# Later x batches load behind the shared weights, high halves move a slot back, batch work is spread over slots, routing in other operations, list values multiplied by GpSimd

## What is computed

```python
def _L0_xattn_ref(x, adj, W, b):          # x is ctx, adj is layernorm(x)
    si = jnp.einsum('bnd,d->bn', x, Wi[0])
    sj = jnp.einsum('bnd,d->bn', x, Wj[0])
    xij = jax.nn.sigmoid(si[:, :, None] + sj[:, None, :] + b[0])
    return P_ASEM * xij + (1.0 - P_ASEM) * adj
...
    probs = jax.nn.softmax(x @ gate_w.T, axis=-1)
    vals, idx = jax.lax.top_k(probs, K)                    # 4 of 16 experts
    w = vals / jnp.sum(vals, axis=-1, keepdims=True)
    ...
    w_gu = dequant_fp4(gate_up_packed, gate_up_scales)
    act = swiglu(jnp.einsum('th,ehi->eti', x, w_gu))
    y_e = jnp.einsum('eti,eih->eth', act, w_d)
    out = jnp.einsum('te,eth->th', combine, y_e)
    act_s = swiglu(x @ dequant_fp4(shared_gate_up_packed, shared_gate_up_scales))
    out = out + act_s @ dequant_fp4(shared_down_packed, shared_down_scales)
...
    x = x + jnp.tanh(g_xattn[0]) * _L0_xattn_ref(ctx_512, _layernorm(x, axis=-1), L0_xattn_W, L0_xattn_b)
    x = x + jnp.tanh(g_ffn[0]) * _L0_ffn_ref(_layernorm(x, axis=-1), ...)
```

## Time and profile before

| | |
|---|---|
| median of 3 runs | 717.2 us (716.89 to 717.4) |
| the profiled execution | 715.78 us |
| its span, first to last instruction | 714.1 us |
| PE busy | 620.8 us, 87% |
| DVE / ACT / POOL busy | 490.2 / 325.8 / 324.8 us |
| mean granted TensorE clock | 0.953 |

### The profile page before, as it was taken

One profiled execution on the slowest core, in us unless ns is written; L12 is line 12 of the kernel. 1 busy time (PEld: TensorE's weight loads), 2 busy tenths in 40 slices (PEclk: granted clock), 3 DMA queues, 4 the chain that ended last, 5 costly groups with the idle time before them and its releaser, 6 DMA issues.

```text
span 714.1 us, 17257 instructions
## 1 busy us (share of the span) xinstructions
PE 620.8 (87%) x4394; PEld 374.8 (52%) x4395; DVE 490.2 (69%) x1271; ACT 325.8 (46%) x558; POOL 324.8 (45%) x506
## 2 busy tenths in 40 slices
PE   3347459995979899999999999999999999999991
PEld 2234236653545456656556566565565556566550
DVE  4695847889857576758778758578678787867110
ACT  1751347632234355455445455454554544554541
POOL 1620354200032456556465475554655646665532
PEclk9759788999899999999999999999999999999997
DMA  6940011204627668584785886758576686754532
GB/s 222 294 139 0 16 45 74 75 1 85 232 53 204 156 143 211 97 210 86 184 187 118 192 175 136 178 106 201 119 180 149 141 204 132 165 88 85 86 40 38
DMA packets 49841, 93.72 MB, mean 131 GB/s; under 512 B 8840, under 2 KB 16776, under 8 KB 49816
## 3 DMA queue, kind: packets, MB, share of 16 engines
q0 software_dynamic: 16128, 38.35, 28.8%
q1 hardware_dynamic: 29464, 49.83, 24.3%
q10 hardware_dynamic: 4224, 5.24, 2.2%
HBM read 65.16 MB, written 28.24 MB: 131 GB/s over the span
## 4 chain that ended last, share of the span: by engine, by line
PE 69%; DVE 13%; DMA 6%; issue 4%; SPq 2%; ACT 2%; POOL 1%; DVEq 1%; POOLq 0%; ACTq 0%
PE gu_ps L1196 41%; PE bank L1224 19%; PE bank L1236 4%; PE bank L1210 4%; DMA dn_sc<-dn_scale_halves 3%; DVE act L987 1%; DMA dn_scale_halves<-wgu 1%; ACT acth L616 1%; DVE stats L721 1%; DVE X L996 1%; DVE mix_room L1023 1%; DVE X L751 1%; PE bank L1180 1%; DVE acth L992 1%; DVE wgu L923 1%
## 5 line engine op out<-in xcount | busy, mean ns | idle before, releaser
L1196 PE MATMUL gu_ps<-wgu,mix_room 128*128 x1728 | 305.4, 327 | 2.4 <-DVE tick L946 1.3
L1196 PEld LDWEIGHTS gu_ps<-wgu,mix_room 128*128 128x128 f16 x1728 | 166.3, 98 | 114.3 <-issue 8.6
L1224 PE MATMUL bank<-wdn,aT 128*128 (+1 forms) x792 | 187.2, 382 | 12.1 <-ACT aT L623 11.5
L623 ACT ACTIVATE aT<-bank 128x768 f16<-128x768 f16 x88 | 71.2, 810 | 130.5 <-PE bank L1210 130.5
L524 POOL DMA_INDIRECT out<-mix_room,idx_s x72 | 121.6, 1689 | 18.5 <-issue 17.9
L1224 PEld LDWEIGHTS bank<-wdn,aT 128*128 128x128 f16 x792 | 77.7, 98 | 97.8 <-ACT aT L623 7.8
L987 DVE SCALAR_TENSOR_TENSOR act<-gu_ps,wslot,sg x72 | 44.5, 618 | 104.5 <-ACT sg L609 91.4
L616 ACT ACTIVATE acth<-act 128x384 f16<-128x384 f32 x88 | 46.0, 523 | 133.0 <-DVE act L987 128.3
L521 POOL COPY idx_s<-room_b 128x1 int32 (+1 forms) x72 | 19.0, 263 | 180.9 <-DMA out<-mix_room,idx_s 117.6
L501 POOL COPY idx_g<-room_b 128x1 int32 (+1 forms) x72 | 58.5, 813 | 75.7 <-DVE tick L857 62.6
L504 POOL DMA_INDIRECT room_b<-token_rows,idx_g x72 | 78.5, 1090 | 10.8 <-issue 1.0
(11 more groups left out here) (161 smaller groups left out, 581.5 us busy)
## 6 DMA issues: line engine op xcount, KB each, us to landing
dn_sc<-dn_scale_halves SPq DMA_DIRECT2D x34, 384.0 KB
dn_raw<-in_L_ffn_down_packed SPq DMA_DIRECT2D x48, 256.0 KB
gu_sc<-gu_scale_halves SPq DMA_DIRECT2D x34, 192.0 KB
X<-in_x ACTq DMA_DIRECT2D x4, 1024.0 KB, 9.6
token_rows<-room_a SPq DMA_DIRECT2D x16, 256.0 KB, 2.0
out<-X SPq DMA_DIRECT2D x4, 1024.0 KB, 11.3
gu_raw<-in_L_ffn_gate_up_packed SPq DMA_DIRECT2D x16, 192.0 KB
gu_raw<-in_L_ffn_gate_up_packed SPq DMA_DIRECT2D x16, 191.9 KB
```

Source lines behind the costliest of these rows:

```text
L623: nc.scalar.activation(aT[:, b].rearrange("p a c t -> p (a c t)"), at_ps, ACT.Copy).then_inc(aT_done, 1)
L1196: mm = nc.tensor.matmul(ps[b][:, 0:I], x(xp * HC + c), wgu[:, w, wp, c, col:col + I], start=(c == 0 and xp == 0 and wp == 0), stop=(c == H ...
L1224: mm = nc.tensor.matmul(y_ps[0 if shared else b][:, :], aT[:, b, ap, t, :], wdn[:, w, wp, t, :], start=(n == 0), stop=(n == 3 * IC - 1))
```

## The change

Six things change.

1. SP issues the scale loads first and the constants after them. VectorE splits the scales before it makes `wj_all`. ScalarE's queue loads ctx 0 and 1, x 0, ctx 2 and 3, and after the scales have landed x 1; the batches 2 and 3 of x are loaded by SP, after all loads of the shared expert have landed and ahead of expert 0's words.
2. GpSimd does the second factors of batch 0 before it scales batch 1, and the low halves of batch 1 before the first 1/std of the batches 2 and 3. VectorE does `attend(0)` before `x_factors(1)`.
3. The high halves of the tiles 8 to 15 are made in the slots 4 to 7 (tiles 2i and 2i+1 in slot i) and stood in the slots 3 to 6 (tiles 2i+2 and 2i+3).
4. The batch work of VectorE is spread over the slots 2 to 8 in another way, and the dequantisation of expert 0 with it (parts in the slots 4, 6, 7, 8 where it was 5 to 8).
5. Routing takes fewer VectorE operations: the scale of the logits goes into ScalarE's exponential, the comparison and the product become one operation, the mask of chosen experts is written as fp16 at once, the counts come out of TensorE in the order in which they are scanned (and the triangle is minus one on and below where it was zero, so that the subtraction goes). Operations that only the routed loops need (`last_tables`, `slot_tables`) come in slot 14 with a tick of their own (`route_ready` 2), the token weights in slot 13 after the marks.
6. In `mark` the product of slots and token numbers is made by GpSimd, before its gathers. TensorE waits for it.

```diff
@@ sync
+            for k, ap in enumerate((sh_gu_scales..., gu_scales..., sh_dn_scales..., dn_scales...)):
+                sp.dma_start(sc_all[:, columns(k)], spread(ap, k)).then_inc(ld_sc, 16)
             for k in range(2):
                 sp.dma_start(wij[:, k:k + 1], ...
...
             load_scales(sp, 0, 0)
+            sp.wait_ge(ld_w[0], 16 * LOADS)
+            for b in range(2, B):
+                sp.dma_start(X[:, b * TB:(b + 1) * TB, :], x_t[b]).then_inc(ld_x[b], 16)
             load_words(sp, gu_packed[0], dn_packed[0], 1)
@@ gpsimd
             inverse_std(0, 1)
-            scaled_x(1)
             inverse_std(1, 0)
             norm_factors(0)
+            scaled_x(1)
             low_halves_x(0)
             inverse_std(1, 1)
             norm_factors(1)
+            low_halves_x(1)
             inverse_std(0, 2)
             inverse_std(0, 3)
-            low_halves_x(1)
             scaled_x(2)
...
+            for j in range(TOP_K):
+                pool.wait_ge(slots_ready, j + 1)
+                nc.gpsimd.tensor_tensor(values[:, j % 2], values[:, j % 2],
+                                        token1[:, :].unsqueeze(2).broadcast_to([P, NT, SLOTS]), ALU.mult).then_inc(values_ready, 1)
+
             pool.wait_ge(rows_zero, 16)
@@ scalar
+            load_ctx(0)
+            load_ctx(1)
+            load_x(0)
+            load_ctx(2)
+            load_ctx(3)
             a.wait_ge(ld_sc, 64)
-            for b in range(B):
-                load_x(b)
+            load_x(1)
...
                 activate(i, i % 2)
+                if 4 <= i < NT // 2:
+                    high_x(2 * i)
                 if i in WITH_X:
                     copy_xT(2 * i - 1)
...
-                if i in WITH_X and 2 * i + 2 < NT:
-                    high_x(2 * i + 2)
-                    high_x(2 * i + 3)
+                if 4 <= i < NT // 2:
+                    high_x(2 * i + 1)
@@ vector, route
-                step(nc.vector.tensor_scalar(lg[:, :, :], lg[:, :, :], 1.0 / (X_SCALE * R_SCALE), None, ALU.mult))
...
-                step(nc.vector.memset(r_keep[:, :, :], 1.0))
-                step(nc.vector.memset(r_keep[:, :, 0:1], 0.0))
...
-                step(nc.vector.tensor_scalar(r_run[:, :, :], r_run[:, :, :], float(TOP_K), None, ALU.is_le))
-                step(nc.vector.tensor_tensor(r_eq[:, :, :], r_eq[:, :, :], r_run[:, :, :], ALU.mult))
-                step(nc.vector.tensor_tensor(r_gt[:, :, :], r_gt[:, :, :], r_eq[:, :, :], ALU.add))
-                nc.vector.tensor_copy(sel16[:, :], ...).then_inc(sel_ready, 1)
+                step(nc.vector.scalar_tensor_tensor(r_eq[:, :, :], r_run[:, :, :], float(TOP_K), r_eq[:, :, :], ALU.is_le,
+                                                    ALU.mult))
+                nc.vector.tensor_tensor(sel, r_gt[:, :, :], r_eq[:, :, :], ALU.add).then_inc(sel_ready, 1)
@@ vector, after_shared_slot
                 if i == 2:
                     first_stats(2)
+                    first_stats(3)
+                if i == 3:
                     x_factors(2)
-                    first_stats(3)
-                    x_factors(3)
-                if i == 3:
                     attend(2)
                     second_stats(2)
+                    x_factors(3)
                 if i == 4:
+                    first_weights(0)
+                if i == 5:
                     attend(3)
                     second_stats(3)
-                if 5 <= i < 9:
+                if i == 6:
+                    first_weights(1)
+                    step(nc.vector.memset(r_keep[:, :, :], 1.0))
+                    step(nc.vector.memset(r_keep[:, :, 0:1], 0.0))
+                if i in (7, 8):
                     first_weights(i - 5)
...
-                if i == 11:
+                if i in (11, 12):
+                    mark(2 * (i - 11))
+                    mark(2 * (i - 11) + 1)
+                if i == 13:
                     token_weights()
-                    mark(0)
-                    mark(1)
-                if i == 12:
-                    mark(2)
-                    mark(3)
+                    lists()
+                if i == NT - 2:
+                    last_tables()
                     slot_tables(0)
-                if i == 13:
                     slot_tables(1)
-                    lists()
```

75 lines of the change are left out of this document (38 added, 37 removed).

## The result

The changed kernel takes 712.56 us (median of 8 runs, 710.96 to 715.58) against 717.05 us for the kernel before on the same chip (8 runs, 715.43 to 718.05). The ratio is 0.9943, with a 95% interval of 0.9926 to 0.9960: faster by 4.5 us (0.6%), where I had forecast 14.5 and a range that ended at 710.

The account below looks back on a forecast made before the run. TensorE's idle time and waits before the routed part, in the first 207.1 us, were to be won: 5.5 + 8 + 1 = 14.5 us off 715.8 gives 701.3, or 702.7 as a median; 8-in-10 range 695 to 710.

Parts of the forecast that it names:

- A: The stretch up to the first gate-up, at 50.80 us before: gain 5.5 us, ends 3 and 9.1.
- B: Slots 2 to 9: gain 8 us, ends 4 and 12.
- C: Slots 10 to 15, routing and marks: gain 1 us, ends −2 (gather 3 us slower beside the load) and 6.
- routed part: From 207.1 us to the end: only moves, 507 us long; expert 1's later load counted as costing 0.
- about 10: Slots 2 to 9: us lost to new gaps (aT of tile 2, slot 4's activation, tiles 8 and 12, clock).
- that wait stays: First gather, before the routed part: TensorE's wait of 2.83 us stays, the gather now sharing DMA engines with expert 1's load.
- (i): Start of the kernel: scale loads move ahead of six constants and start about 2.8 us sooner, at 0.8.
- (ii): Start of the kernel: two of four 1 MB loads of x leave the stretch, saving 6.3 us.
- (iii): Dequantisation before the first gate-up: GpSimd's work beside VectorE stretches its operations, a loss of 3.6 us.
- 7.4 + 7.4 + 3: Slots 2 to 9: gains in us from tile 4's low-half gap, the aT gap of tile 3, and half-clock matmuls.
- strict turns: Marks: GpSimd and VectorE alternate on such operations, so a pair of choices costs 10.6 us where it cost 8.4.
- half gain: Rival, chance 0.17: tile 8's chain costs two full gaps, clock stays low through slots 4 to 6; 7 us gained, 710.

Follow-up runs that it names:

- e11_start_only: The kernel before with only the start's loads reordered (scales first, x 0 and 1 behind them, x 2 and 3 behind the shared weights) and VectorE's split earlier: 710.32 us.
- e4_x0_late: The changed kernel with x 0 loaded behind the landed scales and all four context batches: 710.72 us, ratio 0.9926.
- e5: The changed kernel with batch 2's first 1/std between the low halves of tiles 5 and 6, its factors ending slot 2: 709.36 us, ratio 0.9890.
- e6: The changed kernel with the low halves of tiles 8 and 9 ahead of batch 3's scaling on GpSimd: 710.55 us, ratio 0.9911.
- e12_after_again: The changed kernel timed again, nothing altered: 711.84 us, ratio 0.9938.
- e3: The changed kernel with the token weights back ahead of the marks, in slot 11: 708.28 us, ratio 0.9882.
- e9_load_late: The changed kernel with the token weights ahead of the marks and expert 1's load held until the lists are done: 711.49 us, ratio 0.9935.
- e7_best: The changed kernel with the edits of e4_x0_late, e5, e6 and e3 together: 700.92 us, ratio 0.9782.
- e8_best_product: e7_best with the product of the marks back on VectorE: 700.30 us, ratio 0.9765.
- e10_count_rows: e7_best with the count's matmuls reading the selection in order of memory and the copy of the totals back on VectorE: 701.30 us, ratio 0.9782.
- e2_product_back: The changed kernel with the product of the marks back on VectorE, straight behind the comparison: 713.73 us, ratio 0.9964.

## Why the prediction was wrong, step by step

The direction was right and the size was not: 4.0 us by the spans instead of 14.5, as A 2.8, B 2.0, C −1.6 and routed part +0.8, where I had 5.5, 8, 1 and 0. Three terms failed: the earlier landing of the scales in A, the new gaps of "about 10" in B, and "that wait stays" in C. One of the signs that I had named for wrong came: the shared scales landed after 30, at 30.99.

- **Stage A, (i) failed.** That the scale loads "start about 2.8 us sooner, at 0.8" was right for the issue (0.77), and I took the landing to follow. It came at 10.21 instead of 9.16 (the halves were stored at 13.72 instead of 12.66), since 1 MB of x 0 had been moved ahead as well, in ScalarE's queue. (The Trainium skill, "DMA: Bandwidth & Descriptors", section "Queues, rings and completion order", has the rule: a DMA engine takes packets from its queues in turn. The trace agrees: 8.0 us for the 96 KB beside it, 5.1 without.) What was left of the 2.8 at the reload of the scales was 0.5 us (issued at 20.91 instead of 21.44). (ii) gave 4.9 of 6.3 us: from the reload's issue to the words 10.1 us instead of 14.9. Words at 30.99, not 27.3.
- **Stage A, (iii) right in kind, high in size.** The dequantisation up to the first gate-up took 17.0 us instead of 14.4, 2.5 more, where I had 3.6 for GpSimd beside it. In e11_start_only, with GpSimd's old order, it took 15.4, so about 1.5 of the 2.5 come with the new order of the two engines; the other 1.0 no run separates. With x 0 behind the scales (e4_x0_late) the stage gives 5.6 us, where I had 5.5. That this is so close is partly luck: the words then come 8.1 us sooner (I had 9.1), and 2.5 us are lost again (I had 3.6).
- **Stage B, gains right.** The first gap went from 10.18 to 1.75, that of aT of tile 3 went, and from the first gate-up to slot 5 the kernel gained 17.3 us; my terms (7.4 + 7.4 + 3) are 17.8.
- **Stage B, the loss failed.** I had "about 10" for the new gaps; they came to 15.4 from slot 5 to slot 10, by the starts of the gate-ups (51.6 us instead of 36.3). The activation of slot 4 (3.09, I had 1 to 4.5) and the clock (2.8, "up to 3") were sized right. Too small were tile 8 (4.73, I had 2 to 3) and tile 12 (2.97, I had 1), and a wait of 1.0 us for an activation in slot 9 was not named. Ahead of tile 8 I had GpSimd's scaling of batch 3 at 3.1 us and the low half at 1.2; they took 3.69 and 1.44. For tile 12 no run isolates the cause. The runs e5 and e6 shorten the stretch from the first gate-up to slot 10 from 94.9 us to 92.7 and 92.8 (e12_after_again, the same kernel, has 95.6), and with both B is worth 7.7 us (89.2 us, against 96.9 before). That is the size of the forecast, but in another order of GpSimd's and VectorE's work than the one I had priced.
- **Stage C, marks nearly right.** A pair took 9.5 us, I had 10.6. Read by strict turns, the product's 3.23 us begin with 1.05 of waiting: the row comparison ends at 164.98, the product at 167.16, so its own work is 2.2 us, where I had 2.6. The next comparison (3.61) waits for it until 167.16 and then needs 1.34, where it takes 1.48 alone. All four products ran beside VectorE, so that none shows its own duration directly. So the rows fit the rule (the Trainium skill, "SBUF — State Buffer", terms) to a tenth or two of a microsecond; the estimate by its "GPSIMD Engine Reference", 2.8, was too high. From slot 10 to the last list it took 39.5 us instead of 40.9: 1.4 sooner, I had 1.
- **Stage C, "that wait stays" failed.** The gather took 7.34 us instead of 3.8, and TensorE waited 4.71 instead of 2.83, with a gate-up at a lowered clock behind it (3.19 us instead of 2.11). These 1.9 and 1.1 us against the 1.4 won ahead of them are C's −1.6. This was the low end of my range for C: "the gather 3 us slower beside the load". e3 shows the wait to be the price of `token_weights` behind the marks.
- **The routed part** was as I said: 506.2 us against 507.0. Expert 1's load was in time, by less than a microsecond if it took as long as in e9_load_late.

The nearest rival was the half gain, 710 by A 4, B 4, C −1. It named tile 8's chain and the clock, and was still above each stage. I had given it 0.17. That the four edits of e7_best end at 700.9, close to the forecast's 702.7, is no proof of the forecast: it is another kernel. As I read them, all three misses are of one kind: where the change moved work beside other work, I charged the gain in full and the new company at the cheaper end.

## What to carry to other kernels

A gap that is taken away shows the next chain, so judge a reordering by the last engine that has to serve the following tile: here one line moved alone gave 0.5 us of a 10 us gap, and the whole reordering, with its successors' order mended, 7.7. When a load is issued earlier, ask what is moved ahead with it in other queues: here the scales were issued 2.9 us sooner and landed 1.1 us later, with 1 MB moved ahead beside them. Small work that a later DMA hangs on can be worth placing ahead of long work: here five operations for a 128 KB store, put ahead of the marks, gave some 4 us, although the marks came 2 us later.

## What the chip showed that I had not expected

- A matmul whose moving operand is read with a stride (f16, 128x256, step of 16 elements) took 0.62 us instead of 0.28, and behind two of them TensorE's granted clock fell to half in eight profiled runs of ten, and in none of four without them. Why two kept the clock is open.
- What was won in one place was given back by the clock in another: e8_best_product and e10_count_rows came to the first routed slot 2.3 and 1.3 us sooner than e7_best, and both then ran its first gate-up in 3.1 instead of 2.1 us, behind the same wait of 2.1 us. Why is open.
- The first gather, from its issue to ScalarE's first read, took 3.8 us in the kernel before. Behind the row weights' late store and the queued load it took 6.6 (e4_x0_late), 7.4 (changed; 6.6 in e12_after_again, the same kernel), 8.2 (e6_low_first), 8.7 (e5_factors_early) and 9.3 us (e2_product_back): the same 128 rows, in runs where nothing of it was changed.
